# Windowed attention by head pairs or by tile pairs: sharing one transposed block of probabilities between two query tiles

## The reference, cut to what matters

```python
qc = q.reshape(B, H, nc, W, d)                    # W = 64
scores = einsum('bhcqd,bhckd->bhcqk', qc, kb) / sqrt(d)
allowed = mask & pos_ok & (abs(rel) <= W)         # 3W keys per chunk of W queries
scores = where(allowed, scores, -1e9)
probs = softmax(scores, axis=-1)
out = einsum('bhcqk,bhckd->bhcqd', probs, vb)
```

## Time and profile before

| what | value |
|---|---|
| median of three runs | 1976.86 us (1970.09 to 1981.36) |
| the profiled execution's own time | 1966.12 us |
| its span in the trace | 1964.3 us |
| mean granted TensorE clock | 0.898 |
| TensorE busy | 1532.7 us, 78% |
| VectorE busy | 1340.6 us, 68% |
| ScalarE busy | 1026.9 us, 52% |
| GpSimd busy | 712.5 us, 36% |
| 96 pairs of one banded attention stage | 163.4 to 167.8 us |
| 96 pairs of the full attention stage | 155.2 us |

### The profile page before, as it was taken

One profiled execution on the slowest core, in us unless ns is written; L12 is line 12 of the kernel. 1 busy time (PEld: TensorE's weight loads), 2 busy tenths in 40 slices (PEclk: granted clock), 3 DMA queues, 4 the chain that ended last, 5 costly groups with the idle time before them and its releaser, 6 DMA issues.

```text
span 1964.3 us, 45857 instructions
## 1 busy us (share of the span) xinstructions
PE 1532.7 (78%) x14634; PEld 1290.7 (66%) x14634; DVE 1340.6 (68%) x3638; ACT 1026.9 (52%) x2392; POOL 712.5 (36%) x993
## 2 busy tenths in 40 slices
PE   0689889789798898898897938849818886669992
PEld 0467668677677776786776827729816664569992
DVE  4698966789876989668997662253358998344444
ACT  0478733688534787337884313225417883235661
POOL 5554123553134641236531320024525421045541
PEclk9899989899898999899998968769958997679996
DMA  5645101634004451016430000046526430067775
GB/s 130 185 108 115 28 1 31 163 76 87 1 2 128 85 116 28 1 32 160 88 74 1 1 13 1 1 142 189 168 72 140 85 63 23 22 200 241 239 219 173
DMA packets 144329, 178.46 MB, mean 91 GB/s; under 512 B 22096, under 2 KB 106128, under 8 KB 143952
## 3 DMA queue, kind: packets, MB, share of 16 engines
q1 hardware_dynamic: 136784, 158.18, 31.6%
q0 software_dynamic: 7296, 17.18, 2.6%
HBM read 132.96 MB, written 42.34 MB: 89 GB/s over the span
## 4 chain that ended last, share of the span: by engine, by line
PE 31%; DVE 14%; issue 4%; ACT 2%; DMA 2%; POOL 1%; SPq 0%; DVEq 0%; ACTq 0%; POOLq 0%
PE bank L1414 7%; DVE ptl L772 4%; DVE neg_max L766 2%; PE bank L1400 2%; PE bank L548 2%; PE bank L618 2%; DVE xn L886 1%; PE bank L1403 1%; DMA xn<-y_rows 1%; PE bank L1401 1%; PE bank L1402 1%; PE bank L1404 1%; PE bank L423 1%; PE bank L1158 1%; ACT pth L670 1%
## 5 line engine op out<-in xcount | busy, mean ns | idle before, releaser
L660 ACT ACTIVATE prob<-bank,neg_max 128x192 f32<-128x192 f32 (+1 forms) x960 | 408.1, 436 | 132.2 <-DVE neg_max L766 79.0
L772 DVE TENSOR_TENSOR ptl<-bank,pth 128x512 f16<-128x512 f32 x480 | 327.0, 681 | 11.8 <-ACT pth L670 5.6
L766 DVE TENSOR_REDUCE neg_max<-bank 128x2 f32<-128x384 f32 (+1 forms) x480 | 273.4, 570 | 77.5 <-PE bank L537 68.7
L548 PE MATMUL bank<-ident,prob 128*128 128x128 f32 x1920 | 309.6, 285 | 0.0
L670 ACT ACTIVATE pth<-bank 128x512 f16<-128x512 f32 x480 | 284.8, 593 | 7.8 <-PE bank L548 7.5
L566 PE MATMUL bank<-v,pth 128*128 128x33 bf16 x1920 | 200.8, 181 | 106.7 <-DVE ptl L772 89.6
L566 PEld LDWEIGHTS bank<-v,pth 128*128 128x128 f16 x1920 | 154.7, 96 | 190.5 <-DVE ptl L772 177.5
L625 ACT ACTIVATE xx<-bank 128x256 fp32r<-128x256 f32 x256 | 95.7, 387 | 239.8 <-PE bank L423 235.6
L548 PEld LDWEIGHTS bank<-ident,prob 128*128 128x128 f32 x1920 | 205.1, 142 | 0.1
L568 PE MATMUL bank<-v,ptl 128*128 128x33 bf16 x1920 | 194.9, 177 | 0.0
L567 PE MATMUL bank<-v,pth 128*128 128x16 bf16 x1920 | 191.0, 170 | 1.9 <-issue 1.9
(11 more groups left out here) (281 smaller groups left out, 4078.7 us busy)
## 6 DMA issues: line engine op xcount, KB each, us to landing
xn<-in_e_seg SPq DMA_DIRECT2D x34, 768.0 KB, 6.7
w<-in_e_w SPq DMA_DIRECT2D x23, 576.0 KB, 4.2
qk_rows<-fbuf SPq DMA_DIRECT2D x128, 96.0 KB, 2.3
qx<-qk_rows SPq DMA_DIRECT2D x35, 288.0 KB, 4.1
kx<-qk_rows SPq DMA_DIRECT2D x35, 288.0 KB, 5.7
qk_rows<-w SPq DMA_DIRECT2D x80, 96.0 KB, 2.3
qx<-qk_rows SPq DMA_DIRECT2D x35, 192.0 KB, 4.7
kx<-qk_rows SPq DMA_DIRECT2D x35, 192.0 KB, 5.5
```

The costliest lines, as they stand in the source:

```text
L548: last = nc.tensor.transpose(bank[BT[p % 2]][:, (2 * e + c) * P:(2 * e + c) * P + P], prob[:, qt, hd % PROBS, c * P:c * P + P], ident[:, :])
L660: nc.scalar.activation(prob[:, qt, hd % PROBS, c0:c0 + n], scores_at(u // 2, n)[:, u % 2, :], ACT.Exp, bias=neg_max[:, tile_no % 3, hd:hd ...
L766: nc.vector.tensor_reduce(neg_max[:, t % 3, hd:hd + 2], scores_at(p, D if banded else S), AX.X, ALU.max, negate=True).then_inc(max_ready.s ...
L772: nc.vector.tensor_tensor(ptl[:, p % 2, :], bank[BT[p % 2]][:, :], pth[:, p % 3, :], ALU.subtract)\
```

## The change

A pair becomes both query tiles of one head, at 384 pairs of the banded layers and 96 of the full one. The two tiles' probabilities stand next to each other (192 + 192 columns), and three transposes turn them: the first block is tile 0's first 128 keys, the third tile 1's last 128 keys, and the middle one holds tile 0's last 64 keys in its first 64 rows and tile 1's first 64 keys in its last 64. The copy and the subtraction take 384 columns in place of 512. The values of tile 0 are issued before the transposes of a later pair, those of tile 1 after them; in the banded layers each half waits for the half before it. The product with the middle block uses 64 rows. A bank holds six heads of both tiles, a finish covers those, and tiles come ready two at a time. The full layer keeps four transposes. The probability buffer is a ring of six pairs, and its zero columns are gone.

```diff
 def where(u):
-    return u // (2 * HEADS), u // HEADS % 2, u % HEADS
+    return u // (2 * HEADS), u % 2, u // 2 % HEADS

 def pe_scores(...):
-        nc.tensor.matmul(o, ident_bf, mask[:, 2 * b + qt, :].unsqueeze(1).to_broadcast([P, 2, D]),
-                         start=True, stop=False)
-    for e in range(2):
-        last = nc.tensor.matmul(o[:, e, :], qx[0:ROWS, b % 3, hd + e, qt * P:qt * P + P],
-                                kx[0:ROWS, b % 3, hd + e, ks], ...)
+        nc.tensor.matmul(o, ident_bf, mask[:, 2 * b:2 * b + 2, :], start=True, stop=False)
+    for qt in range(2):
+        last = nc.tensor.matmul(o[:, qt, :], qx[0:ROWS, b % 3, hd, qt * P:qt * P + P],
+                                kx[0:ROWS, b % 3, hd, keys(qt, banded)], ...)

+def turns(banded):
+    return 3 if banded else 4

 def pe_turn_probs(pe, it, p, banded):
-    for e in range(2):
-        _, qt, hd = where(2 * p + e)
-        for c in range(2):
-            last = nc.tensor.transpose(bank[BT[p % 2]][:, (2 * e + c) * P:(2 * e + c) * P + P],
-                                       prob[:, qt, hd % PROBS, c * P:c * P + P], ident[:, :])
+    for c in range(turns(banded)):
+        last = nc.tensor.transpose(bank[BT[p % 2]][:, c * P:c * P + P],
+                                   probs[:, p % PROBS, c * P:c * P + P], ident[:, :])

+def pe_values(pe, it, p, banded, qt):
+    b, _, hd = where(2 * p)
+    if qt == 0:
+        pe.wait_ge(lo_ready.sem, lo_ready.at(it, p + 1))
...
+    if banded:
+        pe.wait_ge((first_half if qt else pv_done).sem, (first_half if qt else pv_done).at(it, p + qt))
+    o = bank[BV[p // 6 % 2]]
+    every_row = slice(0, P)
+    if banded:
+        parts = ((0, 0, every_row), (1, 1, slice(0, P - WIN))) if qt == 0 else \
+            ((2, 1, every_row), (1, 0, slice(P - WIN, P)))
+    else:
+        parts = ((2 * qt, 0, every_row), (2 * qt + 1, 1, every_row))
+    for i, (turn, chunk, rows) in enumerate(parts):
+        w, v = slice(turn * P, turn * P + P), v3[rows, (b // 2) % 2, 2 * (b % 2) + chunk, hd, :]
+        c = (hd % 6 * 2 + qt) * OC
+        o2, o1 = o[:, c:c + OC], o[:, c + 1 + DH:c + OC]
+        nc.tensor.matmul(o2, pth[rows, p % 3, w], v[:, 0:OC], start=i == 0, stop=False)
+        nc.tensor.matmul(o1, pth[rows, p % 3, w], v[:, OC:VC], start=False, stop=False)
+        last = nc.tensor.matmul(o2, ptl[rows, p % 2, w], v[:, 0:OC], start=False, stop=i == 1)
+    last.then_inc((pv_done if qt else first_half).sem, 1)

 def pe_attention(...):
                 if p >= 5:
-                    pe_values(pe, it, p - 5)
+                    pe_values(pe, it, p - 5, banded, 0)
                 if 0 <= p - 3 < PAIRS:
-                    pe_turn_probs(pe, it, p - 3)
+                    pe_turn_probs(pe, it, p - 3, banded)
+                if p >= 5:
+                    pe_values(pe, it, p - 5, banded, 1)

 def act_exp(act, it, u, banded):
-    back = u - PROBS if hd >= PROBS else u - 2 * HEADS + PROBS
-    if back >= 0:
-        act.wait_ge(t_done.sem, t_done.at(it, back // 2 + 1))
+    if qt == 0 and p >= PROBS:
+        act.wait_ge(t_done.sem, t_done.at(it, p - PROBS + 1))

 def act_hi(act, it, p, banded):
-    nc.scalar.activation(pth[:, p % 3, :], bank[BT[p % 2]][:, :], ACT.Copy)
+    n = turns(banded) * P
+    nc.scalar.activation(pth[:, p % 3, 0:n], bank[BT[p % 2]][:, 0:n], ACT.Copy)

 def dve_lo(dve, it, p, banded):
-    nc.vector.tensor_tensor(ptl[:, p % 2, :], bank[BT[p % 2]][:, :], pth[:, p % 3, :], ALU.subtract)
+    nc.vector.tensor_tensor(ptl[:, p % 2, 0:n], bank[BT[p % 2]][:, 0:n], pth[:, p % 3, 0:n], ALU.subtract)

 def dve_finish(dve, ch, it, f, step, banded):
-            finish_marks[0] = ch.mark(nc.vector.scalar_tensor_tensor(
-                rs2[:, 0, :], in0=pad_exp[:, r3, :], scalar=pad_keys[:, t % 2:t % 2 + 1], in1=po[:, :, 0], ...))
+            for qt in range(2):
+                finish_marks[0] = ch.mark(nc.vector.scalar_tensor_tensor(
+                    by_tile(rs2[:, 0, :])[:, :, qt], in0=by_tile(pad_exp[:, b % 2, :])[:, heads, qt],
+                    scalar=pad_keys[:, qt:qt + 1], in1=by_tile(po[:, :, 0])[:, :, qt], ...))
...
-        nc.vector.tensor_tensor(o[:, 0:HEADS, :], au[:, :, :], r, ALU.mult)
-        nc.vector.tensor_tensor(o[:, HEADS:, :], au[:, 8:HEADS, :], r[:, 8:HEADS, :], ALU.mult)
+        last = nc.vector.tensor_tensor(o[:, :, heads, :], x, r, ALU.mult)
+        if half:
+            last = nc.vector.tensor_tensor(o[:, :, HEADS:, :], x[:, :, 2:6, :], r[:, :, 2:6, :], ALU.mult)

 # GpSimd, at the start
-nc.gpsimd.memset(prob[:, 0, :, D:2 * P], 0.0)
-nc.gpsimd.memset(prob[:, 1, :, 0:WIN], 0.0).then_inc(zeroed.sem, 1)
```

More of the change, by code:

```diff
@@ L283, in build_tower @@
         exp_done = sig("exp_done", per=2 * PAIRS)
-        pad_ready = sig("pad_ready", per=NT)
+        pad_ready = sig("pad_ready", per=B)
         t_done = sig("t_done", per=PAIRS)
         hi_ready, lo_ready = sig("hi_ready", per=PAIRS), sig("lo_ready", per=PAIRS)
-        pv_done = sig("pv_done", per=PAIRS)
+        pv_done, first_half = sig("pv_done", per=PAIRS), sig("first_tile_values_done", per=PAIRS)
         att_ready = sig("att_ready", per=NT)
@@ L524, in pe_scores @@
         def pe_scores(pe, it, p, banded):
-            b, qt, hd = where(2 * p)
+            b, _, hd = where(2 * p)
             pe.wait_ge(exp_done.sem, exp_done.at(it, 2 * p - 4))
-            if b == 0 and qt == 0 and hd % 4 == 0:
+            if b == 0 and hd % 4 == 0:
                 pe.wait_ge(first_in[hd // 4].sem, first_in[hd // 4].at(it, 16 * READS))
-            elif b and p % (PAIRS // B) == 0:
+            elif hd == 0:
                 pe.wait_ge(qk_in[b % 3].sem, qk_in[b % 3].at(it, 16 * READS * (b // 3 + (b % 3 > 0))))
-            ks = keys(qt, banded)
@@ L532, in pe_scores @@
-            o = scores_at(p, ks.stop - ks.start)
+            n = D if banded else S
+            o = scores_at(p, n)
             if banded:
-                nc.tensor.matmul(o, ident_bf, mask[:, 2 * b + qt, :].unsqueeze(1).to_broadcast([P, 2, D]),
-                                 start=True, stop=False)
-            for e in range(2):
-                last = nc.tensor.matmul(o[:, e, :], qx[0:ROWS, b % 3, hd + e, qt * P:qt * P + P],
-                                        kx[0:ROWS, b % 3, hd + e, ks], start=not banded, stop=e == 1 or not banded)
+                nc.tensor.matmul(o, ident_bf, mask[:, 2 * b:2 * b + 2, :], start=True, stop=False)
@@ L539, in pe_scores, with pe_turn_probs @@
+            for qt in range(2):
+                last = nc.tensor.matmul(o[:, qt, :], qx[0:ROWS, b % 3, hd, qt * P:qt * P + P],
+                                        kx[0:ROWS, b % 3, hd, keys(qt, banded)], start=not banded,
+                                        stop=qt == 1 or not banded)
             last.then_inc(s_done.sem, 1)
-        def pe_turn_probs(pe, it, p):
+        def turns(banded):
+            return 3 if banded else 4
+        def pe_turn_probs(pe, it, p, banded):
             pe.wait_ge(lo_ready.sem, lo_ready.at(it, p - 1))
@@ L544, in pe_turn_probs @@
             pe.wait_ge(exp_done.sem, exp_done.at(it, 2 * p + 2))
-            for e in range(2):
-                _, qt, hd = where(2 * p + e)
-                for c in range(2):
-                    last = nc.tensor.transpose(bank[BT[p % 2]][:, (2 * e + c) * P:(2 * e + c) * P + P],
-                                               prob[:, qt, hd % PROBS, c * P:c * P + P], ident[:, :])
-            last.then_inc(t_done.sem, 1)
[L552 to L569, removed]
@@ L684, in act_attention @@
                 if 0 <= p - 3 < PAIRS:
-                    act_hi(act, it, p - 3)
+                    act_hi(act, it, p - 3, banded)
                 if p < PAIRS:
@@ L770, in dve_lo, with dve_finish @@
             dve.wait_ge(hi_ready.sem, hi_ready.at(it, p + 1))
             dve.wait_ge(pv_done.sem, pv_done.at(it, p - 1))
-            nc.vector.tensor_tensor(ptl[:, p % 2, :], bank[BT[p % 2]][:, :], pth[:, p % 3, :], ALU.subtract)\
+            n = turns(banded) * P
+            nc.vector.tensor_tensor(ptl[:, p % 2, 0:n], bank[BT[p % 2]][:, 0:n], pth[:, p % 3, 0:n], ALU.subtract)\
                 .then_inc(lo_ready.sem, 1)
         finish_marks = [None, None]
-        def dve_finish(dve, ch, it, t, step, banded):
-            r3, r = t % 3, rs2[:, 1, :]
+        def dve_finish(dve, ch, it, f, step, banded):
+            b, half, r = f // 2, f % 2, rs2[:, 1, :]
+            heads = slice(6 * half, 6 * half + 6)
@@ L1955, in _ @@
         def _(pe):
-            for s in (xt_done, proj_done, s_done, t_done, pv_done, o_done, u_done, y_done, xc_qk_done, xc_v_done,
+            for s in (xt_done, proj_done, s_done, t_done, pv_done, first_half, o_done, u_done, y_done, xc_qk_done, xc_v_done,
                       xc_gram_done, xc_kt_done, xc_pt_done, xc_y_done, xc_o_done, gates_done, r_done, g2_done):
```

69 lines of the change are left out of this document (37 added, 32 removed).

## The result

The changed kernel took 2122.89 us as the median of four runs (2104.86 to 2200.02), beside 1974.64 for four runs of the kernel before. The ratio is 1.0653, with an interval of 1.0607 to 1.0698, some 129 us where 27 were forecast. The forecast was slower, 2004 us in a range of 1945 to 2055: the direction was right, the size and the range were wrong.

A forecast was written before the change was run, and what follows sets the result against it. VectorE's maximum and subtraction mostly bound the banded loop before, TensorE after. 96 pairs of 1.42 us plus 22.8 and idle time gave 172.5 per stage, +27 over four layers: 1993, or 2004 as a median, range 1945 to 2055.

The forecast's parts named there:

- Subtraction, copy, exponentials' wait: Banded pairs: VectorE's subtraction 0.13 us shorter, ScalarE's copy 0.10 us shorter; exponentials lose a buffer wait of 10 us per stage.
- One transpose less: TensorE, banded pairs: three transposes instead of four save 0.11 us per pair, 10.3 us per layer.
- Changes of shape at 0.105 each: TensorE, banded values products: four switches between 64 and 128 rows per pair, 0.105 us each, priced from the router products.
- The bounds above it: TensorE, price of one change between 64 and 128 rows: at most 0.17 us, if the load's 96 ns are bared too.
- rival 3: Banded pairs: each change also bares the half-precision load, 0.14 us, total 2057 us; chance 0.15 together with Rival 4.
- Own waits at nothing: TensorE, banded pairs: two new waits on its own products, covered by transposes and scores, cost nothing.
- Rival 4: Banded pairs: TensorE's waits on its own products are bared, 0.1 us each, 2042 us with one; chance 0.15 with rival 3.
- TensorE becomes the bound, plain pair 1.42: Banded stages: TensorE's plain pair grows from 1.11 to 1.42 us, above VectorE's 0.98 plus extras, so TensorE bounds.
- Stage 172.5 at full clock: Each banded attention stage takes 172.5 us instead of 166.0, including idle time at front, end and where VectorE ends last.
- Full stage 0 to -2 us: The full layer's attention stage keeps four transposes, has no 64-row matmul, and changes by 0 to -2 us.

The follow-up runs named there:

- the two kernels whose clock stayed up: The changed kernel with a useless 384-column mask product per banded pair, 2051.82 us, and the changed kernel with a useless fourth transpose per banded pair, 2060.97 us.

## Why the prediction was wrong in size and right in sign

- **Subtraction, copy, exponentials' wait:** right, at 546 and 488 ns, with the wait for transposes gone.
- **One transpose less:** right as time (0.107 each). What it was worth besides, as activity that kept the clock up, was not in the sum.
- **Changes of shape at 0.105 each:** right, 0.10 over the gap of like shapes (0.128 and 0.125 against 0.025), in both directions and in half precision. The router's rows carried over. The bounds above it were not consistent: a bared load of 96 ns on top of 0.105 makes 0.20, where the prediction wrote 0.17 and rival 3 took 0.14. No run came near any of them.
- **Own waits at nothing:** right; 0.3 us in the second stage after. Rival 4 is out; its price of 0.1 for an uncovered wait was measured nowhere.
- **TensorE becomes the bound, plain pair 1.42:** right at the full clock, 1.39; at half clock it is 2.13.
- **Stage 172.5 at full clock:** near, 170 to 171.5 by the two kernels whose clock stayed up. Over four stages against 166.0 that is +17 to +22 us; +26 was forecast for the stages.
- **Full stage 0 to -2 us:** -2.2, at the edge of the forecast.
- **The step that failed is the sum's unspoken first line: that each of these instructions runs at the clock it had in the trace of before.** Every price was taken from full-clock rows and kept. No rival priced a fall of the clock. Rival 3 reached as far as 2057 with a bared load, which did not happen (a change costs 0.10, not 0.14), and the range stopped at 2055. By the ratio the kernel takes 1.0653 x 1976.86 = 2106 us, where 1993 to 1999 would hold at a full clock. The remaining 107 to 113 us are left for the clock.

What could have been read in the trace of before? Its row of the clock:

```profile
PEclk9899989899898999899998968769958997679996
```

Outside the attention stages it has slices of 5 to 7, so the clock moves in this kernel, and the two levels differ by two. A rival "the banded stages run a third of their pairs at the lower level" was there to be named. Its price, with the lengths of the trace after: an average pair takes 2.61 us in place of 1.75, so a third of 384 pairs is 128 x 0.86 = 110 us. On top of the 2004 forecast that is 2114, near the 2106 by the ratio. The third itself is hindsight; in the traced run it was over half (152 of some 280 pairs), and no row of before could give the share. The Trainium skill (TensorE: Matmul & The Clock Gate, Part 1) describes these two clock levels, and that TensorE's activity moves it between them. The traces agree on the levels (0.50 and 1.00).

What stays open is by what the chip decides. Shown: the fall takes both, the gaps at the changes of shape (without them 0.93 to 0.97) and the sparser work between them (with a 384-column product or one transpose more per pair it is back at 0.96 to 0.99). The busy share of the profile does not tell it: at 6.00 of 6.00 us busy the clock was 1.00 in one piece and 0.50 in another. Whether ordering the products so that each pair has two changes in place of four (both middle products together) would hold the clock was not tried.

## What to carry to other kernels

- Before mixing 64-row and 128-row operands in a stream of short matmuls, count the changes: each was 0.10 us here, several times the 0.025 us in which like-shaped short products follow each other. Laying the halves into one full-height operand, zeros included, cost TensorE nothing here and avoided them; GpSimd paid for the copies (320.0 us busy in the four stages against 276.2), off the bound.
- When a change makes TensorE's stream sparser, price its clock as a rival of its own, at the lower level, and read it stage by stage in the profile after. A high busy share did not vouch for the clock here.
- Useless products are a quick test: the changed kernel got faster with them, and a good part of its loss was in the clock. The remedy to look for first is to remove the gaps.

## What the runs showed of the hardware that was not expected

- The granted clock of TensorE fell to half in stretches where its records are busy for 6.00 of 6.00 us, and over whole stages at 96% busy.
- One f32 transpose more per pair (0.107 us in 1.4) took the stages from clocks of 0.63 to 0.88 to 0.96 to 0.98.
- At half clock a change of shape shows the same distance between loads as at full clock. The second stage, after the change, at clock 0.50:

```profile
560.50 0.11 PEld L578 LDWEIGHTS bank<-v,ptl 128*128 128x128 f16 x1
560.64 0.10 PEld L576 LDWEIGHTS bank<-v,pth 64*128 64x128 f16 x1
...
560.69 0.10 PEld L578 LDWEIGHTS bank<-v,ptl 64*128 64x128 f16 x1
560.83 0.50 PEld L551 LDWEIGHTS bank<-ident,prob 128*128 128x128 f32 x3
```

  0.14 us in and 0.14 out (medians of the stage 0.144 and 0.138, 0.128 and 0.125 at full clock). What gets longer at half clock is the rest, as the three f32 loads (0.50 us, 0.31 at full clock), and with it the pair, 2.13 us for 1.39: less than double.
- A program at the edge of this spreads over 4% from run to run on one chip (2092.34 to 2173.14), where the kernel before beside it spreads over 1%: the spread was a first sign of its cause.
